# Causal mask of query blocks 2 and 3 moved from the matrix engine into the maxima of the vector engine

## The reference

```
xn = layernorm(x)
q, k, v = xn Wq^T, xn Wk^T, xn Wv^T          # 16 heads of 16 columns
scores[h, s, t] = q[h, s] . k[h, t], masked where t > s
attn = softmax(scores / 4);  s = (attn v) Wo^T
g = silu(ffn(xn)),  ffn(x) = (silu(x Wg^T) * (x Wu^T)) Wd^T     # hidden 768, integer weights / 127
out = x + s * g
```

## Time and profile before

| | |
|---|---|
| median of 3 runs | 947.63 us (947.14 to 948.02) |
| span of the profiled execution | 945.8 us |
| PE busy | 914.8 us, 97% |
| DVE busy | 707.2 us, 75%, 950 instructions |
| ACT busy | 585.8 us, 62% |
| POOL busy | 495.1 us, 52% |
| granted TensorE clock | 0.998 |

### The profile page before, as it was taken

One profiled execution on the slowest core, in us unless ns is written; L12 is line 12 of the kernel. 1 busy time (PEld: TensorE's weight loads), 2 busy tenths in 40 slices (PEclk: granted clock), 3 DMA queues, 4 the chain that ended last, 5 costly groups with the idle time before them and its releaser, 6 DMA issues.

```text
span 945.8 us, 22760 instructions
## 1 busy us (share of the span) xinstructions
PE 914.8 (97%) x9065; PEld 685.6 (72%) x9065; DVE 707.2 (75%) x950; ACT 585.8 (62%) x796; POOL 495.1 (52%) x681
## 2 busy tenths in 40 slices
PE   3999999999999999999999999999999999999995
PEld 2777767776868777686877868777786867768654
DVE  5985868778696887868788786877778697776823
ACT  5356664757576675756657575665757557575771
POOL 4253553736456464645636455473745547364553
PEclk9999999999999999999999999999999999999999
DMA  6704235353353534535343453534345253543323
GB/s 221 213 25 170 84 116 169 100 198 132 134 164 127 170 106 179 154 125 171 129 151 126 170 152 117 176 132 158 130 148 162 104 185 120 175 131 135 118 93 98
DMA packets 84507, 133.97 MB, mean 142 GB/s; under 512 B 13680, under 2 KB 34928, under 8 KB 84336
## 3 DMA queue, kind: packets, MB, share of 16 engines
q1 hardware_dynamic: 84400, 132.47, 41.8%
HBM read 53.22 MB, written 25.75 MB: 83 GB/s over the span
## 4 chain that ended last, share of the span: by engine, by line
PE 91%; DVE 2%; DMA 2%; POOL 2%; issue 1%; ACT 1%; SPq 0%; POOLq 0%; ACTq 0%; DVEq 0%
PE bank L194 48%; PE values L525 15%; PE bank L434 12%; PE bank L492 11%; PE bank L447 4%; DMA o_reciprocals<-scratch_r 1%; ACT probs L500 1%; DVE row_max L457 1%; PE bank L463 1%; POOL o_compact L566 1%; PE bank L668 0%; DMA scratch_r<-sum_reciprocals 0%; DVE x_in L259 0%; DVE xt_lo L279 0%; DMA sums<-scratch_o 0%
## 5 line engine op out<-in xcount | busy, mean ns | idle before, releaser
L457 DVE TENSOR_REDUCE row_max<-bank 128x2 f32<-128x768 f32 (+3 forms) x352 | 384.9, 1124 | 63.5 <-PE bank L447 60.3
L500 ACT ACTIVATE probs<-bank 128x1024 f32<-128x1024 f32 x320 | 320.4, 1026 | 122.2 <-PE bank L492 120.8
L507 POOL TENSOR_SCALAR_AFFINE_SELECT probs<-probs 128x256 f32<-128x256 f32 (+1 forms) x448 | 194.0, 450 | 275.1 <-ACT probs L500 274.1
L525 PE MATMUL values<-probs,v 128*17 128x512 f32 (+3 forms) x2048 | 166.2, 436 | 0.9 <-POOL probs L507 0.9
L393 POOL TENSOR_TENSOR h_lo<-gated,h_hi 128x512 fp32r<-128x512 f32 x96 | 124.6, 1298 | 74.8 <-ACT h_hi L390 72.7
L434 PE MATMUL bank<-k_stack,q_stack 64*128 64x128 f32 (+3 forms) x1024 | 155.3, 363 | 1.5 <-DVE row_max L457 1.2
L492 PE MATMUL bank<-q_stack,k_stack 64*128 64x512 f32 (+3 forms) x1024 | 142.2, 350 | 1.3 <-DVE row_max L457 0.7
L434 PEld LDWEIGHTS bank<-k_stack,q_stack 64*128 64x128 f32 x1024 | 83.1, 186 | 66.9 <-issue 30.4
L492 PEld LDWEIGHTS bank<-q_stack,k_stack 64*128 64x128 f32 x1024 | 82.9, 186 | 39.1 <-issue 17.3
L366 DVE SCALAR_TENSOR_TENSOR gated<-gated,bank 128x512 f32<-128x512 f32 x96 | 65.8, 685 | 55.4 <-ACT gated L363 55.4
L194 PE MATMUL bank<-xt_hi,wg_hi 128*128 128x256 f32 x384 | 99.3, 293 | 1.6 <-DVE gated L379 1.6
(11 more groups left out here) (123 smaller groups left out, 1624.4 us busy)
## 6 DMA issues: line engine op xcount, KB each, us to landing
k_stack<-qk_hi SPq DMA_DIRECT2D x64, 256.0 KB, 2.5
q_stack<-qk_hi SPq DMA_DIRECT2D x64, 256.0 KB, 2.5
scratch_o<-o SPq DMA_DIRECT2D x64, 256.0 KB, 2.2
x_again<-x SPq DMA_DIRECT2D x16, 512.0 KB, 4.7
k_stack<-qk_lo SPq DMA_DIRECT2D x32, 256.0 KB, 2.5
q_stack<-qk_lo SPq DMA_DIRECT2D x32, 256.0 KB, 2.6
o_compact<-scratch_o SPq DMA_DIRECT2D x32, 256.0 KB
o_reciprocals<-scratch_r SPq DMA_DIRECT2D x32, 256.0 KB
```

Of the source, the lines that this page charges most:

```text
L457: signal(e.tensor_reduce(rows, scores, axis=AX.X, op=ALU.max), "d_sm")
L500: signal(e.activation(PR[:, (SCORES * beta + k) % SLOTS, :, :], both(banks), ACT.Exp, scale=SCALE_S), "d_ex")
L507: last = e.affine_select(out=diag, in_=diag, compare_op=ALU.is_ge, fill=0.0, base=0, pattern=[[0, many], [1, P]], channel_multiplier=-1)
L525: last = nc.tensor.matmul(PVB[32 * c:32 * c + VW, j * P:S], V[par][:, j, 4 * g + c, :], PR[:, (SCORES * beta + 5 * g + kind) % SLOTS, pari ...
```

## The change

For query blocks 2 and 3 (`i >= MASKED_BY_VECTOR`, which is 2) PE no longer issues the four mask matmuls. The last product matmul of `sm` raises a new semaphore `f_sv`, and DVE waits for that. In the place of one reduce over both heads DVE issues one `tensor_tensor_reduce` for each head: it adds a constant row `CAUSAL` (bf16, zero but for MASKED above the diagonal of its last 128 columns) to the scores, writes the sum back into the PSUM bank, and puts the maximum of the sums into one column of `row_max`. Blocks 0 and 1 stay as they were. POOL fills `CAUSAL` with a memset and an affine_select before it enters its list. The tables of order are the same.

```diff
+MASKED_BY_VECTOR = 2
-    ... f_mt=2, f_sm=22, f_st=20, ...
+    ... f_mt=2, f_sm=6, f_sv=16, f_st=20, ...
+WITH_MASK = [k for k, (i, _) in enumerate(MAXIMA) if i < MASKED_BY_VECTOR]
+WITHOUT_MASK = [k for k, (i, _) in enumerate(MAXIMA) if i >= MASKED_BY_VECTOR]
+        CAUSAL = sb("causal_rows", [P, S], BF16)
...
 u_sm, pe:
+                by_vector = i >= MASKED_BY_VECTOR
-                        nc.tensor.matmul(PS[:, n, j * keys:(j + 1) * keys], ..., start=j == 0, stop=False,
+                        last = nc.tensor.matmul(PS[:, n, j * keys:(j + 1) * keys], ..., start=j == 0, stop=by_vector,
+                if by_vector:
+                    signal(last, "f_sv")
...
 u_mk:
-            if en == "pe":
+            if en == "pe" and not by_vector:
...
             elif en == "dve":
-                after(e, "f_sm", beta, k)
+                if by_vector:
+                    after(e, "f_sv", beta, WITHOUT_MASK.index(k))
+                else:
+                    after(e, "f_sm", beta, WITH_MASK.index(k))
...
+                if by_vector:
+                    if beta == 0:
+                        e.wait_ge(s_causal, 2)
+                    for parity, m in enumerate(banks):
+                        for j in range(n):
+                            scores = PS[:, m, j * keys:(j + 1) * keys]
+                            col = 32 * half + 16 * parity + TT * (at + j) + i
+                            last = e.tensor_tensor_reduce(out=scores, in0=scores, in1=CAUSAL[:, S - keys:S], scale=1.0, scalar=MASKED,
+                                                          op0=ALU.add, op1=ALU.max, accum_out=MX[:, half, col:col + 1])
+                    signal(last, "d_sm")
+                    return
...
 gpsimd, before run("pool", e):
+            e.memset(CAUSAL[:], 0.0).then_inc(s_causal, 1)
+            e.wait_ge(s_causal, 1)
+            e.affine_select(out=CAUSAL[:, S - P:S], in_=CAUSAL[:, S - P:S], compare_op=ALU.is_ge, fill=MASKED, base=0,
+                            pattern=[[-1, P]], channel_multiplier=1).then_inc(s_causal, 1)
```

More of the change, by code:

```diff
@@ L26 @@
 MASKED = -3.0e38
+MASKED_BY_VECTOR = 2
 COUNT = dict(
-    f_gm=3, d_gm=3, f_tr=2, d_xm=1, f_qk=4, f_v=2, f_gg=FT, f_gu=FT, f_dn=2, f_op=2, f_mt=2, f_sm=22, f_st=20, f_pv=12,
+    f_gm=3, d_gm=3, f_tr=2, d_xm=1, f_qk=4, f_v=2, f_gg=FT, f_gu=FT, f_dn=2, f_op=2, f_mt=2, f_sm=6, f_sv=16, f_st=20, f_pv=12,
     d_ln=3, d_rs=1, d_rc=2, d_xn=1, d_xh=2, d_xl=2, d_qh=4, d_ql=4, d_v=2, d_t=FT, d_a=FT, d_h=FT,
@@ L159, in build @@
         s_first = [sem(f"s_first{t}") for t in range(TT)]
-        s_const, s_fixed = sem("s_const"), sem("s_fixed")
+        s_const, s_fixed, s_causal = sem("s_const"), sem("s_fixed"), sem("s_causal")
         s_zeros, s_ones, s_kfill, s_qfill = sem("s_zeros"), sem("s_ones"), sem("s_kfill"), sem("s_qfill")
@@ L433, in u_sm @@
                         low = 64 * parity
[L434 to L437, removed]
+                        last = nc.tensor.matmul(PS[:, n, j * keys:(j + 1) * keys],
+                                                r(QS[par][low:low + STACK, pair, i * P:(i + 1) * P]),
+                                                r(KS[par][low:low + STACK, pair, 0:keys]), start=j == 0, stop=by_vector,
+                                                skip_group_check=True)
+                if by_vector:
+                    signal(last, "f_sv")
         def u_mk(en, e, beta, par, k, banks, prev):
```

## The result

The changed kernel takes 951.12 us (median of 4, 950.43 to 951.7), the kernel before beside it 947.38 us: 1.0044 times as long, 95% interval 1.003 to 1.0058. It is slower, as forecast, but by 3.7 us where I had 20.

A forecast was written before the change was run, and what follows sets the result against it. PE and DVE were taken to pull each other through the maxima, DVE as much the bound as PE in the dense stretch. Span 945.8 + 19.2 + 0.9 = 965.9 us, measured time say 967; range 934 to 1012.

The forecast's parts named there:

- r: On DVE, what the `accum_out` costs for each head; taken as 0.077 us, bounds from nothing to 0.24.
- DVE's heavy parts: Two parts of each batch entry's dense stretch, eight heavy entries each; DVE's dense-stretch windows forecast at 97% or more.
- PE's 0.07 us a block: Mask matmuls removed on PE: at most 18 to 19 us over 256 blocks, counted as buying nothing.
- DVE's term: Dense stretch: 49 us more DVE work, overflowing idle time by 1.46 us, less 0.25: 1.2 a batch entry, 19 us.
- the seams: Earlier `f_sv` and catching up in the light 19.1 us: 0.25 us a batch entry taken off the overflow.
- The start: POOL fills `CAUSAL` ahead of `mv`, which layernorm of the first entry needs: about 0.9 us later, nothing hides it.
- The rival in which both cancel: Overflow absorbed at the seams, PE's saving pays for the rest: 945 to 953 us, chance 0.08.
- the gaining case: Rival: r near nothing, DVE's idle time holds the added work, PE keeps 11 to 18 us: 930 to 938, chance 0.20.

The follow-up runs named there:

- the two halves: Changed kernel without masks of blocks 2 and 3, one DVE reduce, no `CAUSAL`: 935.61 us; kernel before with DVE also adding zeros: 960.18 us.

## Why the prediction was wrong

The direction held, and so did several of the marks by which I wanted to be judged: 1024 matmuls fewer, a read-out of its own for each head with r at about 0.06 us (I took 0.077), DVE's heavy parts busy for 98%. Others failed: DVE's busy time rose by 31 us and not by 49, a period is 55.8 us and not 57, and the weight loads' waits for `row_max`, of which I had counted 34, are 55 us and not over 60 (66 only with PE's own row). The size failed at one step of the sum, and with it the picture of PE behind it.

**The failed step** is "PE's 0.07 us a block buys nothing more, because in both parts PE then waits for banks". I counted the removed matmuls at nothing; measured alone they are worth 12 to 13 us of the 18 to 19. The rows for it were there: the waits of PE's weight loads for `row_max` came 33 and 16 times, 49 times in 16 batch entries, so in 3 places of each. And these 34 us were no loss of PE's: nearly all of them passed while its matmuls ran, and PE's own idle time for `row_max` was 1.9 us in 4 places, against 11.8 in 33 after the change. I read the microseconds of the weight loads and DVE's busy share of the stretch and took PE to be held everywhere in it. A share of 92% says that DVE has little idle time, not that PE waits for it at each step.

**DVE's term** came near by luck, by two errors that work against each other. I had 49 us more work. Measured from the start of each of the 256 entries to the next instruction, or to its own end where DVE then stood idle, it was 34, from 265.5 to 299.9 us. With the next one ready, an entry costs 0.15 us more (1.14 to 1.29, 0.87 to 1.01), not 0.19; and only 38 entries in place of 103 now end in idle time, where an entry costs its full row. Of the 49 us I let the first 25 vanish in idle time, and 4 at the seams. In truth a third to a half of the work lands, although only 0.92 us of the idle time in a batch entry was used up (0.89 and 0.69 before, 0.30 and 0.36 after). Probably that idle time doesn't lie where the overrun is; no run shows it. I had 19 us; 12 us measured with the masks kept, 15.5 without them (935.6 to 951.1), of which 0.9 is the start.

**The start.** `mv` comes at 9.99 us in place of 9.11, 0.9 later as forecast. In the profiled pair this does not arrive at PE, whose first transpose starts at 13.74 and before at 13.99, but that is chance, for the reason under the last heading. Where that reason acts alike the term was right: 13.63 and 13.74 us against 12.72 and 12.75 without the fill, and 14.75 to 14.94 against 13.99.

**The sum again**, with what was measured: -12 to -13 for PE, +14.6 for DVE's work with the masks gone, +0.9 for the start: 3 us, against 3.7 measured. This is no test, since the 14.6 is itself read from the changed kernel's time; the two halves measured each alone make about 0. The rival in which both cancel was there at 0.08, with 945 to 953 us, and I gave it too little, since I had no price for the part of PE's saving that stays. By one profiled pair 1.5 us of the loss lie in the stretches with maxima; with the start's 0.9 this leaves about 1 us of the 3.7, which is not separated from noise. The low end of my range also leaves out half of the gaining case (930 to 938), and not the third that I wrote.

## What to carry to other kernels

When work leaves a busy engine, ask in how many places it waits for another one and whether it stands idle there: here the idle time between PE's matmuls told more than the waits of its weight loads, most of which lay behind running matmuls. With little of it, a good part of the saving was kept. When work is added to a partner engine that is nearly full in a stretch, neither "hidden in its idle time" nor "one for one" is right; here about half landed at first and three quarters later. And before moving work between two engines that hold each other, ask whether it is needed at all: the mask in the maxima was not.

## What the runs showed of the hardware

An add-and-max of VectorE on 128x512 fp32 in PSUM, written back in place, takes 0.73 us and steps of 0.65, with its read-out row of 0.14; a plain maximum over the same 512 columns takes 0.68 us (156.4 us of busy time in 256). One fill of one column adds 0.01 us or less to an entry of block 3, three add 0.05 or more.

DVE instructions were held up beside POOL's. At the start four DVE instructions on `x_in` (SBUF to SBUF, 128x256) take 3.76 us when POOL's CAST starts 0.04 us after them, as before the change, and 2.64 when it starts 0.39 us after them, as in the changed kernel:

```profile
11.05 2.64 DVE L263 TENSOR_SCALAR x_in<-x_in,mv 128x256 f32<-128x256 f32 x4 [5.18 <-POOL mv L241]
11.44 1.46 POOL L667 CAST probs<-probs 128x1536 f32<-128x1536 int32 x1 [0.42 <-DMA probs<-wgT]
```

In the twelve traces there are seven of the first kind and five of the second: 3.6 to 3.8 us where the CAST starts between 0.08 us ahead and 0.13 us after, 2.5 to 2.6 us where it starts 0.37 us after or later. The CAST waits for the transfer of the weights, whose landing so moves PE's first transpose by 1.2 us, from 12.7 to 13.99 without the fill and from 13.7 to 14.9 with it. In the same way a DVE instruction of four columns, `var`, lasts until POOL's instruction beside it is done:

```profile
558.02 1.29 POOL L588 TENSOR_TENSOR o_compact<-o_compact,o_reciprocals 128x512 f32<-128x512 f32 x1 [1.31 <-DMA o_reciprocals<-scratch_r]
...
558.47 0.86 DVE L237 TENSOR_SCALAR var<-mv 128x4 f32<-128x4 f32 x1
```

It ends at 559.33, POOL at 559.31. In the kernel before, the same row takes 0.17 us in the ten places where none of POOL's had begun before it, and 1.17 to 1.27 us in the six where one began just before it. That the two engines share something is inferred from these times; no run changed POOL's work to test it.
